# Attention and mixture-of-experts block on one core: the output projection, the next row's k product and VectorE's output sum each placed one head later

## The chip, the cores and the metric

The kernel runs on one core of a Trainium2 chip. The metric is the device time of one execution in microseconds (us). The time of the kernel before is the median of three timed runs; beside it stands one profiled execution, whose trace is what all rows below come from.

## The reference, cut to what matters

The input is x of 8 rows (batch entries) of 256 tokens with 256 features.

```python
x = L0_attn_x                                   # (8, 256, 256)
x = x + layernorm(attn(layernorm(x)))           # 16 heads of 16 features
x = x + layernorm(ffn(layernorm(x)))            # top-1 of 8 experts, and a shared one

def attn(x):
    ct_q, ct_kv = lin(x, w_down_q, b_down_q), lin(x, w_down_kv, b_down_kv)
    q = lin(ct_q, w_up_q, b_up_q) + rope(lin(ct_q, wq_r, bq_r))
    k = lin(ct_kv, w_up_k, b_up_k) + rope(lin(ct_kv, wk_r, bk_r))
    v = lin(ct_kv, w_up_v, b_up_v)
    probs = softmax(q @ k.T / 4)                # per head, 256 x 256
    return lin(probs @ v, wo, bo)               # the output projection
```

What the change touches is the line `lin(probs @ v, wo, bo)` of one row, the layernorm over it, the sum into x and the statistics of the second layernorm, and the down-projection (ct_q, ct_kv) of a later row.

## The kernel before, in words

**Two stages.** The first half of the span is attention, the second half the feed-forward part (shared expert, routed experts, final sums). They overlap only at the seam, in the last row's slot. The change lies in attention.

**Slots and heads.** Attention goes through eight slots, one for each row b (`run_attention`, `run_slot`, lines 378 to 411). A slot has 16 heads, h = 0 to 15. In each slot the engines work on several rows at once, as the table AHEAD (line 317) says: stage B (first layernorm and down-projection) on row b+3, A (q and k, rope) on row b+2, N (v) and the M0 step on row b+1, the scores "SM" and the M1 step on row b+1, the exponentials of the heads themselves on row b, D (output projection, layernorm, sum) on row b-1, E (second layernorm, transposition, router) on row b-2. A step whose row doesn't exist is left out: D is absent from slot 0, B from slots 5 to 7. The last slot (b = 7) is written out by hand in the tables `last` and isn't touched by the change.

**The order is written by hand.** Each engine has a table `order` that maps a head to the steps issued behind it. An engine runs its own list strictly in that order, and the lists meet only in semaphores. TensorE (PE), at each head: the transposed scores of head h (L1535, for the exponentials), the scores "SM" number h for the row maxima (L1476), the steps of `order[h]`, and behind heads 3, 7, 11 and 15 a product of probabilities and v (L1515, `quad`). VectorE (DVE), at each head: the row maximum of SM h (a reduction over a 128x512 bank, L1020, 2 elements out), then its own `order[h]`. ScalarE (ACT): the exponential of head h (L849), then its `order[h]`. GpSimd (POOL) has no work by head, only its steps in order.

**Buffers.** The SM scores go through two banks, so SM u waits until reduction u-2 is done (line 1473). The transposed scores also have two banks, so head h waits for the exponential of head h-2 (line 1533). One bank, w2, is used in turn by the transpositions of the attention output (D_avT0, D_avT1, D_aT), by the output projection D_wo (`d_wo`, lines 1574 to 1579, which adds to `wo_ps`) and by the M0 step. VectorE empties it in `d_wo` (lines 1036 to 1045): the sum with the bias (L1040, adds to `y_ready`), then the statistics (`ln_head`, L954 and L958, and L1044). M0 on TensorE (`m_turn`, lines 1481 to 1498) transposes the split row maxima of row b+1 into the same bank; for rows from 2 on it waits for `y_ready` (line 1494), which is the sum of the same slot.

**What follows the output sum.** The chain goes over three engines: VectorE's sum and statistics (step D_y), GpSimd's power to get 1/sqrt (L620, `D_power` at head 12), VectorE's norm (`d_yn`, L1050, step D_yn), GpSimd's sum into x (L654, `D_x1` at head 13), VectorE's statistics of the new x (`d_stats`, L1054 to L1059, step D_stats), GpSimd's second power (`D_power2` at head 15), VectorE's second norm (`d_xn2`, L1067, step E_xn2, at head 0 of the next slot), and behind it on VectorE the reduction of head 1 and the rope product of row b+2 (`rope`, L988, step A_T at head 1). TensorE needs that rope product for A_QK (L1414 to L1420) at head 2, and the second norm for E_xn2T (L1353) at head 3.

**The M0 path.** M0 on TensorE at head 12, then ScalarE's copy out of the bank (`mT_out`, L832, at head 13) and a small DMA into the stack rows (L835); TensorE waits for that DMA at head 0 of the next slot (line 1529).

**The down-projection.** `a_ct` (B_ct, line 1372) makes the first half (the q side) of the down-projection, `ct_half(b, 1)` (B_ct1) the second; ScalarE's copy of both stands behind head 14.

SyncE issues the DMAs of the q and k stacks and of the expert weights; none of its steps is in the change.

Of the kernel before, what the change touches and what calls it, by code (L numbers as in the profile page):

```python
# [115 lines left out]
def program(nc, x, const, w_down, w_q, w_kv, w_rope, w_out, w_router, bias_col, bias_v, bias_o,  # L116
# [6 lines left out]
    with ExitStack() as ctx:  # L123
# [289 lines left out]
        def nothing(*_):  # L413
            return None
# [509 lines left out]
        def _(dve):  # L924
# [146 lines left out]
            def d_router(b, par):  # L1071
# [7 lines left out]
                "D_div0": divide(0), "D_div1": divide(1), "D_y": d_wo, "D_yn": d_yn, "D_stats": d_stats,  # L1079
                "E_xn2": d_xn2, "E_router": d_router}  # L1080
            order = {0: ("E_xn2",), 1: ("A_T",), 2: ("B_stats",), 3: ("B_norm",), 5: ("E_router",),
                     6: ("D_div0",), 8: ("D_div1",), 9: ("N_v",), 11: ("D_y",),
                     12: ("D_yn",), 14: ("D_stats",)}


            done = [0]
# [257 lines left out]
        def _(pe):  # L1344
# [252 lines left out]
            def d_router(b, par):  # L1597
                pe.wait_ge(sm["xn2T_sb"], b + 1)
                for t in range(TB):
# [7 lines left out]
                     "SM": sm_scores, "M0": lambda b, par: m_turn(b, par, 0),  # L1607
                     "M1": lambda b, par: m_turn(b, par, 1), "D_avT0": av_turn(0), "D_avT1": av_turn(1),
                     "D_aT": a_turn, "D_wo": d_wo, "E_xn2T": d_xn2T, "E_router": d_router}
            order = {0: ("A_R",), 1: ("A_Q",), 2: ("M1", "A_QK",), 3: ("E_xn2T",), 5: ("E_router",),  # L1610
                     6: ("D_avT0",), 8: ("D_avT1", "N_v",), 9: ("D_aT", "B_xnT",), 10: ("D_wo",),
                     12: ("M0", "B_ct",), 13: ("B_ct1",)}

            def ranks(n, par):

# [242 lines left out]
```

## Time and profile before

| what | value |
|---|---|
| timed runs | 449.51, 455.03, 458.82 us (median 455.03) |
| the profiled execution | 447.09 us, with a span of 445.3 us |
| mean granted clock of TensorE in it | 0.979 of full |
| TensorE busy over the span | 414.5 us (93%) |
| VectorE busy | 254.7 us (57%) |
| ScalarE busy | 197.8 us (44%) |
| GpSimd busy | 132.9 us (30%) |

The busy times are means over two stages with different limits: attention ends at about 223 us, and behind it VectorE and ScalarE are much less in use. The granted clock is 1.00 at full speed (2.4 GHz) and 0.50 at the lower level (1.2 GHz). In a timeline row the first number is the start in us from the span's start, the second the duration; a number in brackets is how long the engine sat idle before it and what it waited for. Matmuls overlap, so what a group of them costs is best read from the start of one row to the start of the next.

### The profile page before, as it was taken

To read this page: it belongs to the slowest core of one execution; us is meant where nothing else is said; L and a number is where in the kernel's file an instruction comes from. 1 tells how busy PE (TensorE), PEld (TensorE's weight loads), DVE (VectorE), ACT (ScalarE), POOL (GpSimd) and SP (SyncE) were. 2 spreads that over 40 slices of the span, in tenths; PEclk is the share of its full clock that TensorE was granted. 3 is DMA by queue.
4 is the path that set the end of the run, shared out by engine and by line. 5 is a ranking of instruction groups with operands and counts; after the bars stand their busy time and mean duration, and the time that the engine had idled before them with its cause. 6 is when DMAs were issued, how large, how long until landed. Compare 5 with 4: busy or idle time off the path is not lost.

```text
span 445.3 us, 8888 instructions
## 1 busy us (share of the span) xinstructions
PE 414.5 (93%) x3211; PEld 311.8 (70%) x3211; DVE 254.7 (57%) x601; ACT 197.8 (44%) x375; POOL 132.9 (30%) x186
## 2 busy tenths in 40 slices
PE   6998989999999999797989999999999999999990
PEld 5654656676776767374859999999996344489990
DVE  4655378787878777776655782322222334326685
ACT  1634557667676758556541123444444433211110
POOL 1404231516252524303302002222222010016872
PEclk9998899999999999899999999999999999999996
DMA  8899136364544636350067621111111111113432
GB/s 257 194 99 119 33 90 192 84 189 117 160 143 104 195 88 208 100 170 25 27 208 243 211 73 37 36 49 49 49 47 49 49 47 27 37 52 106 143 99 87
DMA packets 51138, 47.77 MB, mean 107 GB/s; under 512 B 5399, under 2 KB 45847, under 8 KB 51095
## 3 DMA queue, kind: packets, MB, share of 16 engines
q1 hardware_dynamic: 44752, 38.29, 32.3%
q0 software_dynamic: 1728, 4.72, 3.8%
q10 hardware_dynamic: 4614, 4.19, 2.8%
q8 instruction: 26, 0.43, 0.4%
q14 instruction: 18, 0.14, 0.1%
HBM read 25.44 MB, written 8.91 MB: 77 GB/s over the span
## 4 chain that ended last, share of the span: by engine, by line
PE 76%; DVE 10%; issue 5%; POOL 4%; ACT 2%; DMA 2%; DVEq 0%; POOLq 0%; ACTq 0%
PE bank L1349 41%; PE bank L1666 6%; PE bank L1353 6%; PE bank L1515 5%; PE bank L1535 5%; PE bank L1476 4%; PE bank L1683 3%; DVE nmax L1020 2%; PE bank L1414 2%; PE bank L1462 1%; POOL x_sb L654 1%; DVE wall L1050 1%; PE bank L1406 1%; DVE stats_at L954 1%; DMA x_sb<-x 1%
## 5 line engine op out<-in xcount | busy, mean ns | idle before, releaser
L1020 DVE TENSOR_REDUCE nmax<-bank 128x2 f32<-128x512 f32 x112 | 74.3, 685 | 33.4 <-PE bank L1476 33.2
L1226 DVE TENSOR_TENSOR stacks<-stacks,bank 128x512 f32<-128x512 f32 x36 | 24.7, 686 | 69.1 <-PE bank L1349 61.5
L1349 PE MATMUL bank<-stacks,wall 128*128 128x128 f32 x512 | 61.2, 276 | 0.4 <-ACT stacks L885 0.4
L1349 PEld LDWEIGHTS bank<-stacks,wall 128*128 128x128 f32 x512 | 59.8, 192 | 2.5 <-issue 1.8
L849 ACT ACTIVATE pv<-bank 128x512 f32<-128x512 f32 x64 | 38.4, 602 | 36.6 <-PE bank L1535 35.6
L1349 PE MATMUL bank<-wall,stacks 128*128 128x256 f32 (+1 forms) x224 | 53.0, 380 | 0.0
L685 POOL DMA_INDIRECT stacks<-x_sc,row_i x20 | 22.2, 1112 | 100.6 <-PE bank L1353 81.6
L885 ACT ACTIVATE stacks<-bank 128x512 f32<-128x512 f32 x36 | 21.5, 597 | 68.3 <-PE bank L1349 57.3
L849 ACT ACTIVATE wall<-bank 128x512 f32<-128x512 f32 x64 | 38.4, 605 | 29.5 <-PE bank L1535 28.5
L1535 PE MATMUL bank<-stacks 99*128 99x256 bf16 x256 | 49.9, 277 | 0.3 <-DMA stacks<-mT 0.3
L1476 PE MATMUL bank<-stacks 96*128 96x256 bf16 x224 | 42.7, 275 | 7.2 <-DVE nmax L1020 7.2
L1349 PEld LDWEIGHTS bank<-stacks,pv 128*128 128x128 f32 x384 | 44.7, 192 | 1.4 <-issue 0.9
L1349 PE MATMUL bank<-stacks,pv 128*128 128x128 f32 x384 | 44.9, 275 | 0.7 <-ACT stacks L879 0.7
L1349 PEld LDWEIGHTS bank<-wall,stacks 128*128 128x128 f32 x224 | 40.5, 190 | 4.4
L1535 PEld LDWEIGHTS bank<-stacks 99*128 99x128 bf16 x256 | 21.6, 101 | 23.4 <-issue 12.8
L1476 PEld LDWEIGHTS bank<-stacks 96*128 96x128 bf16 x224 | 20.5, 98 | 14.6 <-DVE nmax L1020 11.9
L1666 PE MATMUL bank<-pv,stacks 128*64 128x512 f32 x64 | 30.4, 599 | 0.0
L1666 PE MATMUL bank<-wall,stacks 128*64 x64 | 30.4, 599 | 0.0
L1353 PE MATMUL bank<-cst,wall 128*128 128x128 f32 x160 | 24.0, 276 | 3.2 <-DVE wall L979 2.2
L700 POOL DMA_INDIRECT pv<-y_exp,back_i x16 | 16.1, 1004 | 32.5 <-DMA y_exp<-stacks 28.5
L1353 PEld LDWEIGHTS bank<-cst,wall 128*128 128x128 f32 x160 | 17.9, 140 | 6.8 <-issue 3.8
L894 ACT ACTIVATE pv<-wall 128x1024 f32 x20 | 21.2, 1058 | 3.2 <-DVE eid_i L1204 1.8
(198 smaller groups left out, 699.1 us busy)
## 6 DMA issues: line engine op xcount, KB each, us to landing
wall<-gate_up SPq DMA_DIRECT2D x8, 1024.0 KB, 5.4
stacks<-parts_k SPq DMA_DIRECT2D x72, 64.0 KB, 2.6
stacks<-parts_q SPq DMA_DIRECT2D x72, 64.0 KB, 2.5
wall<-down SPq DMA_DIRECT2D x8, 512.0 KB, 6.7
y_exp<-stacks ACTq DMA_DIRECT2D x20, 128.0 KB, 1.7
x_tok<-wall SPq DMA_DIRECT2D x8, 256.0 KB, 2.5
stacks<-x_tok SPq DMA_DIRECT2D x16, 128.0 KB, 2.6
out<-stacks SPq DMA_DIRECT2D x8, 256.0 KB, 2.1
```

The lines of the kernel that those rows point to most:

```text
L685: pool.indirect_dma_start(out=xl[:, par, :], out_offset=None, in_=x_sc, in_offset=bass.IndirectOffsetOnAxis(ap=row_i[:, s - R0:s - R0 + 1] ...
L849: act.activation(probs[h // QUAD % 2][:, h % QUAD, :], st_bank[h % 2][:, :], ACT.Exp, scale=SCALE).then_inc(sm["exp_done"], 1)
L885: act.activation(sg, fg[:, :], ACT.Silu).then_inc(sm["sg_sb"], 1)
L894: act.activation(to, of, ACT.Copy).then_inc(sm["w_second"], 1)
L1020: dve.tensor_reduce(nmax[:, half, qt, 2 * pair:2 * pair + 2], two(sm_bank[u % 2]), AX.X, ALU.max, negate=True).then_inc(sm["sm_max"], 1)
L1226: dve.tensor_tensor(to, sg, fu[:, :], ALU.mult).then_inc(sm["h_sb"], 1)
L1349: last = pe.matmul(out_ap, lhsT, rhs, start=(n == 0), stop=(n == len(pairs) - 1))
L1353: return pe.transpose(out_ap, in_ap, ident)
L1476: last = pe.matmul(two(sm_bank[u % 2])[:, c, :], stacks[0:ROWS, par, 0, place(h), P * qt:P * qt + P], stacks[0:ROWS, par, 1, place(h), :], ...
L1515: last = pe.matmul(two(av_bank)[32 * c:32 * c + 32, g % 2, :], v_aug[:, par, k, QUAD * g + c, :], probs[g % 2][:, c, S * k:S * k + S], sta ...
L1535: last = pe.matmul(two(st_bank[h % 2])[:, k, :], stacks[0:MROWS, par, 1, place(h), P * k:P * k + P], stacks[0:MROWS, par, 0, place(h), :], ...
L1666: last = pe.matmul((fg, fu)[r][U * n:U * n + U, :], xT[:, p, P * k + U * n:P * k + U * n + U], w, start=(k == 0), stop=(k == KT - 1))
```

## The change

Two `order` tables are edited, TensorE's and VectorE's. No instruction is added, removed or resized, and the tables of ScalarE, GpSimd and SyncE stay as they are.

- TensorE: D_wo from behind head 10 to behind head 11 (the twelfth). B_ct from behind head 12, where it stood after M0, to behind head 13, so that both halves of the down-projection stand together there. M0 stays behind head 12.
- VectorE: D_y from behind reduction 11 to behind reduction 12, D_yn from 12 to 13, D_stats from 14 to 15.

```diff
@@ VectorE @@
             order = {0: ("E_xn2",), 1: ("A_T",), 2: ("B_stats",), 3: ("B_norm",), 5: ("E_router",),
-                     6: ("D_div0",), 8: ("D_div1",), 9: ("N_v",), 11: ("D_y",),
-                     12: ("D_yn",), 14: ("D_stats",)}
+                     6: ("D_div0",), 8: ("D_div1",), 9: ("N_v",), 12: ("D_y",),
+                     13: ("D_yn",), 15: ("D_stats",)}
@@ TensorE @@
-            order = {0: ("A_R",), 1: ("A_Q",), 2: ("M1", "A_QK",), 3: ("E_xn2T",), 5: ("E_router",),
-                     6: ("D_avT0",), 8: ("D_avT1", "N_v",), 9: ("D_aT", "B_xnT",), 10: ("D_wo",),
-                     12: ("M0", "B_ct",), 13: ("B_ct1",)}
+            order = {0: ("A_R",), 1: ("A_Q",), 2: ("M1", "A_QK",), 3: ("E_xn2T",), 5: ("E_router",), 6: ("D_avT0",),
+                     8: ("D_avT1", "N_v",), 9: ("D_aT", "B_xnT",), 11: ("D_wo",),
+                     12: ("M0",), 13: ("B_ct", "B_ct1")}
```

## Rows read from the trace of the kernel before

**Rows 1.** Windows over slot 3: window, its length, busy time by engine, granted clock, DMA.

```profile
110.30:134.00 23.70, 23.13 (x201) 16.50 (x200) 18.91 (x46) 16.29 (x35) 9.68 (x17) 1.00 0.51 147
```

**Rows 2.** Timeline of TensorE, slot 3 from head 10, into slot 4.

```profile
126.02 0.38 PE L1476 MATMUL bank<-stacks 96*128 96x256 bf16 x2
126.24 1.97 PE L1349 MATMUL bank<-wo_sb,wall 128*128 128x256 f32 x8
...
128.27 0.38 PE L1476 MATMUL bank<-stacks 96*128 96x256 bf16 x2
128.58 1.07 PE L1515 MATMUL bank<-wall,pv 128*32 128x256 f32 x16
...
129.81 0.38 PE L1476 MATMUL bank<-stacks 96*128 96x256 bf16 x2
130.13 0.28 PE L1496 MATMUL bank<-idb,mparts 128*24 128x128 bf16 x2
130.34 1.13 PE L1349 MATMUL bank<-wall,wd_sb 128*128 128x256 f32 x4
131.31 0.38 PE L1535 MATMUL bank<-stacks 99*128 99x256 bf16 x2
...
133.05 0.38 PE L1535 MATMUL bank<-stacks 99*128 99x256 bf16 x2
133.71 0.39 PE L1476 MATMUL bank<-stacks 96*128 96x256 bf16 x2 [0.27 <-DVE nmax L1020]
...
135.03 0.39 PE L1535 MATMUL bank<-stacks 99*128 99x256 bf16 x2
...
138.80 0.48 PE L1414 MATMUL bank<-wall,wq_sb 64*128 64x256 f32 x1 [0.33 <-DVE rope_t L988]
```

**Rows 3.** Timeline of VectorE, the same stretch.

```profile
128.69 0.69 DVE L1020 TENSOR_REDUCE nmax<-bank 128x2 f32<-128x512 f32 x1 [1.55 <-PE bank L1476]
129.30 0.68 DVE L1040 TENSOR_TENSOR wall<-bank,bo_sb 128x512 f32<-128x512 f32 x1
...
132.17 0.88 DVE L1050 SCALAR_TENSOR_TENSOR wall<-wall,mv_at,rstd_at 128x256 f32<-128x256 f32 x2 [0.22 <-POOL rstd_at L620]
...
134.43 0.75 DVE L954 BATCH_NORM_STATS2 stats_ff<-x_sb 128x6 f32<-128x256 f32 x2 [0.18 <-POOL x_sb L654]
...
135.68 1.28 DVE L1020 TENSOR_REDUCE nmax<-bank 128x2 f32<-128x512 f32 x2
136.88 0.87 DVE L1067 SCALAR_TENSOR_TENSOR wall<-x_sb,mv,rstd 128x256 f32<-128x256 f32 x2
...
138.27 0.47 DVE L988 SCALAR_TENSOR_TENSOR rope_t<-bank,bcol,cst 128x256 f32<-128x256 f32 x1
```

**Rows 4.** Timeline of GpSimd: the second power of slot 3.

```profile
135.85 0.71 POOL L620 TENSOR_TENSOR rstd<-var_ff,neg_half 128x2 f32<-128x2 f32 x1 [1.46 <-DVE var_ff L1058]
```

**Rows 5.** Chain that ended last, into slot 3: the M0 path's DMA.

```profile
108.85 2.74 DMA stacks<-mT
```

**Rows 6.** Timeline of TensorE: head 15 of slot 0.

```profile
63.88 0.39 PE L1476 MATMUL bank<-stacks 96*128 96x256 bf16 x2 [0.20 <-DVE nmax L1020]
```

**Rows 7.** Timeline of TensorE, slot 6 and the first transposition of slot 7.

```profile
196.29 1.99 PE L1349 MATMUL bank<-wo_sb,wall 128*128 128x256 f32 x8 [0.25 <-ACT wall L856]
...
199.89 0.38 PE L1476 MATMUL bank<-stacks 96*128 96x256 bf16 x2
...
203.78 0.39 PE L1476 MATMUL bank<-stacks 96*128 96x256 bf16 x2 [1.08 <-DVE nmax L1020]
...
207.61 0.66 PE L1353 MATMUL bank<-cst,wall 128*128 128x128 f32 x4 [0.57 <-DVE wall L1067]
```

**Rows 8.** Timeline of VectorE: the output sum of slot 6.

```profile
199.37 0.68 DVE L1040 TENSOR_TENSOR wall<-bank,bo_sb 128x512 f32<-128x512 f32 x1
```

**Rows 9.** Windows behind the waits of slots 5 and 6: clock is the third column from the right.

```profile
181.00:185.00 4.00, 3.78 (x27) 1.74 (x28) 2.82 (x9) 0.92 (x3) 2.32 (x6) 0.57 0.35 87
...
203.80:206.00 2.20, 2.20 (x30) 1.09 (x34) 1.84 (x7) 0.51 (x2) 0.74 (x2) 1.00 0.00 0
```

## The prediction, made before the change was run

> **What bounds the kernel now.** I read the windows by slot first, then the timelines of TensorE, VectorE and GpSimd over one slot, then TensorE's waits and the granted clock. In slot 3 TensorE is busy 23.13 of 23.70 us and VectorE 18.91 [rows 1]: the slot is TensorE's, with little room. Two rows show where it still waits: SM 15 started 0.66 us behind its head (133.05 to 133.71) for reduction 13, 0.44 more than the 0.22 that a pair of score products takes from start to start (126.02 to 126.24), and A_QK in the next slot sat idle 0.33 for the rope product [rows 2]. The second matters more. The rope product is the end of a chain that begins with the output sum and hops over VectorE and GpSimd: sum at 129.30, norm at 132.17 (released by GpSimd), statistics at 134.43 (released by GpSimd), second norm at 136.88, rope at 138.27 [rows 3], A_QK at 138.80 [rows 2]. Slots 1 to 4 are alike in this. So each slot has two paths of nearly equal length, TensorE's own list and this chain, and the change moves the chain's start.
>
> **The change part by part.** No instruction comes or goes, and no DMA is issued by a moved step itself; every cost is a wait.
>
> *D_wo one head later.* Between SM 10 (126.02) and the product behind head 11 (128.58) [rows 2] the same instructions now run in another order: head 11 and its scores, then D_wo. What comes after stays at its times: SM 12 at 129.81, M0 ready to run at 130.13 [rows 2]. Cost by itself 0; SM 11 starts at about 126.46 instead of 128.27, which nobody needs early. VectorE's idle time of 1.55 before reduction 11 [rows 3] doesn't vanish, it moves in front of reduction 12.
>
> *The new wait at M0.* M0 overwrites the bank that the output sum reads, and waits for that sum. Before, the sum ended at 129.98 (129.30 + 0.68) [rows 3], just ahead of M0 at 130.13: hidden. Now the sum is queued behind reduction 12. Reduction 11 started 0.42 behind its scores (128.27 to 128.69) and the sum 0.61 behind that [rows 2, 3]; so reduction 12 starts at 129.81 + 0.42 = 130.23, the sum at 130.84, and it ends at 131.52. With 0.04 to wake an engine (SM 11 ended at 128.65, reduction 11 started at 128.69) M0 runs at 131.56, a stall of 1.43. Its bounds are 0 (the old order) and the 1.43 itself: the statistics behind the sum aren't waited for. Queued behind M0 on TensorE is everything else, head 13 first; for that head ScalarE waits, and for the scores VectorE.
>
> *Both halves at head 13.* B_ct no longer stands behind M0 but behind SM 13. It moves no sum on TensorE in slots 1 to 4, and it lets head 13 and SM 13 start right behind the late M0. ScalarE's copy stands behind head 14 as before: 0. In slot 0, where there is no output sum and two scores run per head, TensorE waits for reductions at the last scores (0.20 at 63.88 [rows 6]); B_ct ran under such waits and now comes behind head 13. Bounds 0 and one half product, 0.97 (130.34 to 131.31 [rows 2]); I take 0.5, the middle, as part of it still lies under waits.
>
> *The M0 path's DMA.* It took 2.74 [rows 5] and head 0 of the next slot waits for it. ScalarE issues it behind the exponential of head 13, which moves from 131.31 [rows 2] to about 131.8 (M0 and its 0.21), so the landing moves by about 0.5, while head 0 moves by 1.43 less the 0.44 that SM 15 no longer waits, 0.99: still hidden.
>
> *The chain from the sum to the rope, in slots 1 to 4.* The sum starts 1.54 later (130.84 against 129.30). The norm follows 2.87 behind the sum and the statistics 2.26 behind the norm, both released by GpSimd [rows 3], so these distances stay: 133.71 and 135.97. The second norm came 2.45 behind the statistics, with two reductions (15 and the next 0, 1.28) in between [rows 3]; now reduction 15 stands ahead of the statistics and one is left, so GpSimd's second power decides: it ended at 136.56 (135.85 + 0.71) [rows 4], 2.13 behind the statistics, so the second norm comes at 135.97 + 2.13 + 0.04 = 138.14. Rope 1.39 and A_QK 1.92 behind that [rows 2, 3]: 140.06 against 138.80, that is **+1.26**. TensorE alone would be there sooner: 1.43 of stall, less the 0.44 at SM 15 and the 0.33 at A_QK, +0.66. The chain is late by 0.60 more, and it decides. Four slots: 5.0. Bounds per slot: 0.66 and 1.43.
>
> *Slots 5 and 6* have no down-projection. D_wo there waited 0.25 for ScalarE; behind head 11 it doesn't, which puts SM 12 at 199.64 instead of 199.89, reduction 12 at 200.06 and the sum at 200.67, against 199.37: 1.30 later [rows 7, 8]. M0 stalls there too, but SM 15, which waited 1.08 for a reduction behind the norm, now gets it before the norm: TensorE wins that back at head 15. It gains nothing by it, since the next slot waits for the second norm at the first transposition, 0.57 idle at 207.61 [rows 7]: with the chain 1.3 later, that is +1.3 from slot 6 to 7. From slot 5 to 6 the old run lost time to the clock (0.57 of full in 181 to 185, a loss of 1.7) [rows 9], and I take 0 there, with bounds of -1.7 (all of that loss) and +1.3.
>
> Sum: 0.5 + 5.0 + 0 + 1.3 = 6.8 us. Behind slot 7 TensorE is busy nearly throughout, so it arrives at the end. The profiled execution of 447.09 would be 453.9. The three timed runs lie higher, at a median of 455.03 with 9.3 between them, and I add the sum to that median: **461.8**, 1.5% slower.
>
> **A rule weighed against the rows.** Behind the two waits of slot 5 TensorE ran at 0.57 of full clock for 4 us, a loss of 1.7; behind the same two waits in slot 6 (203.78 is the second) it stayed at 1.00 [rows 7, 9]. So a wait of about a microsecond can cost the clock or not. The Trainium skill, page "TensorE: Matmul & The Clock Gate", section "A second HAM failure mode: psum-queue depth-cycling", says that short idle times between groups of matmuls, often repeated, make the clock swing between its two levels. The trace agrees in slot 5 and not in slot 6; by the rule each new M0 stall is such a gap, and the result is the first rival below.
>
> **Rivals.**
>
> 1. *The clock falls behind the M0 stalls.* For: slot 5 of before [rows 9]; the stall of 1.43 in one piece is longer than any of the waits there. Against: slot 6, and the long busy stretches on either side of the stall in slots 1 to 4. A drop loses 1.7 us, of which 0.60 lies under the rope's wait: 1.1 for each of four slots, 6.8 + 4.4 = 11.2, time 466.2.
> 2. *Not slower: the rope isn't late.* If the chain's distances of rows 3 shrink because GpSimd and VectorE overlap better than I count (power and norm were both seen waiting), TensorE's list alone decides: 4 x 0.66 = 2.6, slot 0 0.5, and slots 5 and 6 keep up to the 1.08 that TensorE gains at head 15, and slot 5's lost clock of 1.7 comes back: 2.6 + 0.5 - 2.2 - 1.7 = -0.8, time 454.2. It decides once the second norm comes 0.60 earlier than I have it. Against: each hop was released by GpSimd in the rows, and none of these operations changed.
> 3. *Stall without the rest.* If nothing is won back by the waits that go, each slot pays its whole stall: 0.5 + 4 x 1.43 + 2 x 1.3 = 8.8, time 463.8. It is inside the forecast's own range.
>
> **How the numbers follow.** Forecast with rival 3: 0.57, for a time from 459 to 464. Rival 1: 0.22. Rival 2: 0.14. For what I haven't seen: 0.07, of it 0.03 on the fast side. A difference of 2% (9.1 us) is about what a measurement of this kernel can tell from no change. Slower by over 2%: most of rival 1 (0.18), the upper end of the forecast (0.04) and half of the unseen (0.04), 0.26. Faster by over 2%: 0.03. Within: 0.71. The range goes from rival 2 with some of the runs' spread, 453, to above rival 1, 469; the likeliest case's own range is 459 to 464.
>
> **What would show it.** Right: in TensorE's timeline M0 idle some 1.4 us behind SM 12 in slots 1 to 4, released by the sum (L1040); no wait at SM 15; A_QK still waiting for the rope; slots 1 to 4 each 1.3 longer; VectorE idle over 2 in front of reduction 12. Wrong: M0 without a wait, slots as long as before or shorter, or a clock below 1.00 behind the stalls (rival 1).

## The result, and the profile after

The changed kernel took 464.81 us, the median of six runs (456.88 to 468.50); the kernel before, run beside it, 452.33 (six runs, 448.01 to 458.82). The ratio is 1.0221, with a 95% interval from 1.0159 to 1.0283: slower, and whether by more than 2% stays open, since 2% lies inside the interval. The ratios here and below compare only those executions of a kernel that lie within 1.5% of its fastest, so this one is lower than the 1.0276 of the two medians. The forecast was 461.8, with a range from 453 to 469.

The profiled execution has a span of 464.4 us, 19.1 more than before. To see where, I cut both spans at the same instructions. These are TensorE's timeline rows of the kernel before at A_QK (the first L1414 of a slot) in slots 0, 1 and 5 and at the first transposition of slot 6; the one of slot 7 is in [rows 7].

```profile
48.70 0.48 PE L1414 MATMUL bank<-wall,wq_sb 64*128 64x256 f32 x1
...
68.58 0.48 PE L1414 MATMUL bank<-wall,wq_sb 64*128 64x256 f32 x1
...
162.56 0.48 PE L1414 MATMUL bank<-wall,wq_sb 64*128 64x256 f32 x1 [0.33 <-DVE rope_t L988]
...
187.07 0.60 PE L1353 MATMUL bank<-cst,wall 128*128 128x128 f32 x4
```

The same instructions in the changed kernel, with the transposition of slot 7:

```profile
55.13 0.48 PE L1414 MATMUL bank<-wall,wq_sb 64*128 64x256 f32 x1
...
75.59 0.48 PE L1414 MATMUL bank<-wall,wq_sb 64*128 64x256 f32 x1
...
174.42 0.48 PE L1414 MATMUL bank<-wall,wq_sb 64*128 64x256 f32 x1 [0.36 <-DVE rope_t L988]
...
199.52 1.06 PE L1353 MATMUL bank<-cst,wall 128*128 128x128 f32 x4
...
226.71 0.66 PE L1353 MATMUL bank<-cst,wall 128*128 128x128 f32 x4 [0.69 <-DVE wall L1067]
```

| stretch | before | after | more |
|---|---|---|---|
| start to A_QK of slot 0 (ahead of every edited step) | 48.70 | 55.13 | 6.43 |
| to A_QK of slot 1 (the edit in slot 0) | 19.88 | 20.46 | 0.58 |
| to A_QK of slot 5 (the edits in slots 1 to 4) | 93.98 | 98.83 | 4.85 |
| to the first transposition of slot 6 | 24.51 | 25.10 | 0.59 |
| to the first transposition of slot 7 | 20.54 | 27.19 | 6.65 |
| to the end of the span | 237.69 | 237.69 | 0.00 |

The first line isn't the change's: nothing edited has run by then. It and most of the fifth are TensorE's clock, as windows of the changed kernel show (the granted clock is the third column from the right):

```profile
30.00:44.00 14.00, 14.00 (x44) 8.39 (x40) 3.74 (x6) 4.63 (x10) 3.38 (x3) 0.52 0.87 100
...
198.00:212.00 14.00, 13.63 (x80) 8.95 (x81) 6.26 (x12) 4.92 (x9) 1.06 (x6) 0.52 0.50 158
...
222.00:226.00 4.00, 4.00 (x34) 1.36 (x26) 2.82 (x9) 1.81 (x4) 2.16 (x4) 0.60 0.01 3
```

TensorE ran both 14 us stretches at nearly half clock (the 1.2 GHz level), and was busy throughout in one and nearly so in the other. The third row is a shorter fall, of some 3 us, just ahead of the transposition of slot 7. In the profiled execution of before the first two windows stood at 0.90 and 1.00. The stretch from 30 to 44 us comes in traces of other kernels too, among them one that has a single edit far behind it (below), and the profiled execution after happens to have it.

Now the slots themselves. TensorE's timeline of the changed kernel in slot 3, which answers to [rows 2]:

```profile
135.47 0.38 PE L1476 MATMUL bank<-stacks 96*128 96x256 bf16 x2
...
136.13 1.89 PE L1349 MATMUL bank<-wo_sb,wall 128*128 128x256 f32 x8
137.95 1.07 PE L1515 MATMUL bank<-wall,pv 128*32 128x256 f32 x16
138.95 0.39 PE L1535 MATMUL bank<-stacks 99*128 99x256 bf16 x2
139.18 0.38 PE L1476 MATMUL bank<-stacks 96*128 96x256 bf16 x2
141.04 0.27 PE L1496 MATMUL bank<-idb,mparts 128*24 128x128 bf16 x2 [1.47 <-DVE wall L1040]
141.24 0.39 PE L1535 MATMUL bank<-stacks 99*128 99x256 bf16 x2
...
144.08 0.38 PE L1476 MATMUL bank<-stacks 96*128 96x256 bf16 x2
...
149.46 0.48 PE L1414 MATMUL bank<-wall,wq_sb 64*128 64x256 f32 x1 [0.36 <-DVE rope_t L988]
```

M0 (L1496) now sits idle for 1.47 and names the output sum (L1040) as what it waited for. SM 15 (144.08) waits no longer. A_QK still waits for the rope product, as before. VectorE in the same stretch, which answers to [rows 3]:

```profile
139.60 0.69 DVE L1020 TENSOR_REDUCE nmax<-bank 128x2 f32<-128x512 f32 x1 [2.43 <-PE bank L1476]
140.21 0.68 DVE L1040 TENSOR_TENSOR wall<-bank,bo_sb 128x512 f32<-128x512 f32 x1
...
143.09 0.88 DVE L1050 SCALAR_TENSOR_TENSOR wall<-wall,mv_at,rstd_at 128x256 f32<-128x256 f32 x2 [0.22 <-POOL rstd_at L620]
...
145.35 0.75 DVE L954 BATCH_NORM_STATS2 stats_ff<-x_sb 128x6 f32<-128x256 f32 x2
...
147.53 0.88 DVE L1067 SCALAR_TENSOR_TENSOR wall<-x_sb,mv,rstd 128x256 f32<-128x256 f32 x2 [0.23 <-POOL rstd L620]
...
148.93 0.48 DVE L988 SCALAR_TENSOR_TENSOR rope_t<-bank,bcol,cst 128x256 f32<-128x256 f32 x1
```

The idle time in front of the reduction ahead of the sum went from 1.55 to 2.43. From the sum on, the hops are 2.88, 2.26 and 2.18 to the second norm and 1.40 to the rope, nearly as forecast from the old rows (2.87, 2.26, 2.17, 1.39). The whole path from SM 10 to the next A_QK took 12.78 before (126.02 to 138.80) and takes 13.99 now (135.47 to 149.46): 1.21 more.

### The profile page after: what moved, and what is told of

Its sections match the earlier page's. It is cut to its first block, busy times and chain, and to the rows that moved or that the text cites. A ratio compares the mean times of both kernels' runs of the same rounds, so it can differ in the third digit from the quotient of the medians.

```text
span 464.4 us, 8888 instructions
## 1 busy us (share of the span) xinstructions
PE 427.8 (92%) x3211; PEld 320.4 (69%) x3211; DVE 255.8 (55%) x601; ACT 197.9 (43%) x375; POOL 133.1 (29%) x186
## 4 chain that ended last, share of the span: by engine, by line
PE 74%; DVE 9%; issue 7%; POOL 5%; DMA 2%; ACT 1%; ACTq 0%; DVEq 0%; POOLq 0%
PE bank L1349 38%; PE bank L1666 6%; PE bank L1353 6%; PE bank L1515 6%; PE bank L1535 5%; PE bank L1476 4%; PE bank L1683 3%; DMA wkv_sb<-w_kv 2%; PE bank L1414 2%; DVE nmax L1020 2%; POOL x_sb L654 2%; PE bank L1462 1%; DVE wall L1050 1%; DVE stats_at L954 1%; POOL rstd L620 1%
## 5 line engine op out<-in xcount | busy, mean ns | idle before, releaser
L1349 PE MATMUL bank<-stacks,wall 128*128 128x128 f32 x512 | 61.2, 276 | 0.4 <-ACT stacks L885 0.4
L1349 PEld LDWEIGHTS bank<-stacks,wall 128*128 128x128 f32 x512 | 59.8, 192 | 2.5 <-issue 1.8
L1349 PE MATMUL bank<-wall,stacks 128*128 128x256 f32 (+1 forms) x224 | 53.0, 380 | 0.0
L1535 PE MATMUL bank<-stacks 99*128 99x256 bf16 x256 | 51.9, 287 | 0.8 <-DMA stacks<-mT 0.7
L1476 PE MATMUL bank<-stacks 96*128 96x256 bf16 x224 | 43.8, 280 | 3.3 <-DVE nmax L1020 3.3
L1349 PEld LDWEIGHTS bank<-stacks,pv 128*128 128x128 f32 x384 | 44.7, 192 | 1.4 <-issue 0.9
L1349 PE MATMUL bank<-stacks,pv 128*128 128x128 f32 x384 | 44.9, 275 | 0.7 <-ACT stacks L879 0.7
L1349 PEld LDWEIGHTS bank<-wall,stacks 128*128 128x128 f32 x224 | 40.5, 190 | 4.4
L1476 PEld LDWEIGHTS bank<-stacks 96*128 96x128 bf16 x224 | 21.5, 100 | 9.5 <-DVE nmax L1020 6.3
L1353 PE MATMUL bank<-cst,wall 128*128 128x128 f32 x160 | 25.1, 286 | 1.6 <-DVE wall L1067 0.7
L1353 PEld LDWEIGHTS bank<-cst,wall 128*128 128x128 f32 x160 | 19.1, 147 | 5.2 <-issue 2.0
```

Of the source, the lines that this page charges most:

```text
L1349: last = pe.matmul(out_ap, lhsT, rhs, start=(n == 0), stop=(n == len(pairs) - 1))
L1353: return pe.transpose(out_ap, in_ap, ident)
L1476: last = pe.matmul(two(sm_bank[u % 2])[:, c, :], stacks[0:ROWS, par, 0, place(h), P * qt:P * qt + P], stacks[0:ROWS, par, 1, place(h), :], ...
L1535: last = pe.matmul(two(st_bank[h % 2])[:, k, :], stacks[0:MROWS, par, 1, place(h), P * k:P * k + P], stacks[0:MROWS, par, 0, place(h), :], ...
```

## The experiments

Two questions were open: which edit costs the time, the stall at M0 or the chain behind the sum; and whether the clock in slot 6 is the change's doing. The table gives the lengths from A_QK to A_QK, read off TensorE's timeline of each kernel.

| kernel | slot 0 to 1 | 1 to 2 | 2 to 3 | 3 to 4 | 4 to 5 |
|---|---|---|---|---|---|
| before | 19.88 | 22.72 | 23.74 | 23.76 | 23.76 |
| the change | 20.46 | 23.93 | 24.97 | 24.97 | 24.96 |
| VectorE's steps alone | 19.87 | 24.37 | 25.40 | 25.39 | 25.40 |
| TensorE's moves alone | 20.46 | 22.04 | 23.64 | 23.09 | 23.08 |
| M0 behind head 13 | 20.45 | 23.91 | 24.94 | 24.94 | 24.95 |
| down-projection alone | 20.45 | 22.73 | 23.98 | 23.76 | 23.76 |
| statistics back | 20.46 | 24.20 | 25.25 | 25.24 | 25.25 |
| D_wo alone | 19.87 | 22.34 | 23.77 | 23.15 | 23.12 |

**VectorE's three steps alone.**

```diff
-                     6: ("D_div0",), 8: ("D_div1",), 9: ("N_v",), 11: ("D_y",),
-                     12: ("D_yn",), 14: ("D_stats",)}
+                     6: ("D_div0",), 8: ("D_div1",), 9: ("N_v",), 12: ("D_y",),
+                     13: ("D_yn",), 15: ("D_stats",)}
```

> Only VectorE's three steps one head later; TensorE's order as before. Chain theory: the sum is behind reduction 12 all the same, M0 waits 1.5 us in each of slots 1 to 6, and B_ct behind M0 delays the scores of head 13, so that VectorE's norm comes some 0.3 later still: slots 1 to 4 longer by 1.5 each, slot 0 unchanged, in all 7 to 9 us slower. Rival (the moves on TensorE cost the time): slots 1 to 4 within 0.3 of before and the time within 2 us of it.

465.91 us, ratio 1.0367 (1.0332 to 1.0403). Slots 1 to 4 are 1.64 longer, slot 0 isn't, and M0 waits as in the changed kernel. So VectorE's steps bring the cost. They lose 0.43 more per slot than the whole change does. The first half of the down-projection stands between M0 and the scores of head 13 here, and VectorE's timeline in slot 3 shows reduction 13 waiting for those scores, ahead of the norm:

```profile
146.03 0.69 DVE L1020 TENSOR_REDUCE nmax<-bank 128x2 f32<-128x512 f32 x1 [0.57 <-PE bank L1476]
146.64 0.87 DVE L1050 SCALAR_TENSOR_TENSOR wall<-wall,mv_at,rstd_at 128x256 f32<-128x256 f32 x2
```

The norm comes 3.24 behind the sum (143.40) instead of 2.88, which is 0.36 of the 0.43. In time I expected 7 to 9 us more and got 16.4 (465.91 against 449.56 beside it), a miss. Its trace had lost 9.3 ahead of every edit (A_QK of slot 0 at 57.96 against 48.70) and lost 3.1 from the transposition of slot 6 to that of slot 7 (23.68 against 20.54), with half clock in both stretches. So the slots give the price of the edit, and the ratio doesn't.

**TensorE's moves alone.** The `order` table of TensorE from the change, VectorE's as before.

> Only TensorE's moves (D_wo behind head 11, both halves of the down-projection behind head 13); VectorE's order as before, so the sum waits for D_wo right behind reduction 11. Chain theory: the sum starts about 0.7 earlier than before (128.55 in the times of the trace before), M0 doesn't wait, the rope product isn't late, slots 1 to 4 shorter by 0.3 (if the DMA behind M0 then holds head 0) to 0.8, slot 0 longer by 0.6: 0.6 to 2.6 us faster than before. Rival (the moves on TensorE cost the time): 5 us or more slower.

447.61 us, ratio 0.9865 (0.9828 to 0.9903): faster than before, and by more than the 0.6 to 2.6 us expected. With D_wo behind SM 11 reduction 11 comes early, and the sum follows D_wo's end directly. TensorE's moves aren't the cost; one of them gains. VectorE's timeline of this kernel, at the output sum of slot 3, shows that the sum now waits for D_wo (L1349) and no longer for scores:

```profile
131.18 0.69 DVE L1040 TENSOR_TENSOR wall<-bank,bo_sb 128x512 f32<-128x512 f32 x1 [0.88 <-PE bank L1349]
```

Slots 1, 3 and 4 are shorter by 0.67 to 0.68, slot 2 by 0.10 only: a DMA of the next row's stacks holds its end (0.72 idle at 114.46). The expectation left out slots 5 and 6, and more of the gain lies there: 22.64 against 24.51 from A_QK of slot 5 to the first transposition of slot 6, and 19.53 against 20.54 to that of slot 7. A part of the first is the clock that the kernel before lost in its slot 5 [rows 9].

**M0 behind head 13.** The whole change, with M0 moved past the stall:

```diff
-                     12: ("M0",), 13: ("B_ct", "B_ct1")}
+                     13: ("B_ct", "B_ct1", "M0")}
```

> The whole change, but M0 behind the down-projection at head 13 instead of behind head 12, so that the wait for the sum is covered by 1.9 us of work. Stall theory (what TensorE loses at M0 is what the change costs): slots 1 to 4 back to within 0.3 of before, the time 5 to 6 us under the changed kernel. Chain theory (the sum's late start is carried to the rope product): M0 waits for nothing, TensorE is early at head 15, waits about 1.3 more for the rope product, and slots 1 to 4 stay 1.0 to 1.3 longer: the time within 2 us of the changed kernel.

460.11 us, ratio 1.0280 (1.0229 to 1.0331). This is the run that parts stall and chain. TensorE's timeline in slot 3 of this kernel:

```profile
133.93 1.89 PE L1349 MATMUL bank<-wall,wd_sb 128*128 128x256 f32 x8
135.75 0.28 PE L1496 MATMUL bank<-idb,mparts 128*24 128x128 bf16 x2
...
138.88 0.39 PE L1535 MATMUL bank<-stacks 99*128 99x256 bf16 x2 [0.49 <-DMA stacks<-mT]
...
142.88 0.28 PE L1496 MATMUL bank<-idb,mparts 128*24 128x128 bf16 x2 [0.77 <-POOL mparts L648]
143.51 0.48 PE L1414 MATMUL bank<-wall,wq_sb 64*128 64x256 f32 x1 [0.36 <-DVE rope_t L988]
```

M0 at 135.75 waits for nothing; the 1.47 are gone in slots 1 to 4 (in slots 5 and 6, without a down-projection to cover it, 1.03 are left). Yet slots 2 to 4 are 24.94 or 24.95, within 0.03 of the change. The time came back as other waits further on: 0.49 for M0's own DMA at head 0, and 0.77 instead of 0.19 for GpSimd ahead of M1. Behind these A_QK still waits 0.36 for the rope product, as in the change. The chain on VectorE shows why:

```profile
134.29 0.68 DVE L1040 TENSOR_TENSOR wall<-bank,bo_sb 128x512 f32<-128x512 f32 x1
...
137.16 0.88 DVE L1050 SCALAR_TENSOR_TENSOR wall<-wall,mv_at,rstd_at 128x256 f32<-128x256 f32 x2 [0.22 <-POOL rstd_at L620]
...
139.42 0.75 DVE L954 BATCH_NORM_STATS2 stats_ff<-x_sb 128x6 f32<-128x256 f32 x2 [0.18 <-POOL x_sb L654]
...
141.59 0.88 DVE L1067 SCALAR_TENSOR_TENSOR wall<-x_sb,mv,rstd 128x256 f32<-128x256 f32 x2 [0.23 <-POOL rstd L620]
...
142.99 0.47 DVE L988 SCALAR_TENSOR_TENSOR rope_t<-bank,bcol,cst 128x256 f32<-128x256 f32 x1
```

Its hops are 2.87, 2.26, 2.17 and 1.40, within 0.01 those of the change, so A_QK comes no earlier. The stall theory had the slots near 23.75. The stall at M0 is where TensorE loses the time in the changed kernel, and not what fixes the slot's length.

The time by itself would have misled: 460.11 is 4.7 under the 464.84 that the changed kernel took beside it, nearer to what the stall theory said (5 to 6 under) than to the chain theory's 2. In the traces that gain isn't in slots 1 to 4. It lies ahead of every edit (A_QK of slot 0 at 49.27 against 55.13) and from the transposition of slot 6 to that of slot 7 (22.72 against 27.19), and both are stretches with less half clock.

**The down-projection's first half alone, and the statistics back at head 14.**

```diff
@@ on the kernel before @@
-                     12: ("M0", "B_ct",), 13: ("B_ct1",)}
+                     12: ("M0",), 13: ("B_ct", "B_ct1")}
@@ on the changed kernel @@
-                     13: ("D_yn",), 15: ("D_stats",)}
+                     13: ("D_yn",), 14: ("D_stats",)}
```

> Of the change only the down-projection's first half behind head 13. Chain theory: slot 0 is longer by 0.57 as in the changed kernel, slots 1 to 4 within 0.1 of before. Rival (standing behind the stall is what lets the scores of head 13 go first, so the move is worth something by itself): slots 1 to 4 shorter by 0.2 or more.

> The whole change, but VectorE's statistics of the new x stay behind reduction 14. Chain theory: two reductions stand between the statistics and the second norm again, so the norm comes 2.45 instead of 2.17 behind the statistics, as in the trace before, and slots 1 to 4 are longer by a further 0.2 to 0.3. Rival (moving the statistics is a cost of its own): slots 1 to 4 shorter than with the change.

The first took 457.52 in a single execution and made slot 0 longer by 0.57 and three of the four other slots by nothing (slot 2 by 0.24, with a wait of 0.45 for a DMA at its end). It is the whole of slot 0's term, and no gain elsewhere. The second took 465.02, also once; its slots 1 to 4 are 0.28 longer than with the change. That is the difference of 2.45 and 2.17 between statistics and second norm: with two reductions between them the norm is behind VectorE's list, with one behind GpSimd's power.

**The changed kernel again, and with its waits filled.** First the same kernel once more:

> The changed kernel once more, to part what the change does in every execution from what the clock does in some. In the first trace of it TensorE ran at 0.50 from about 31 to 44 us, ahead of every edited step, and again from about 198 to 211 us in slot 6. Theory 1 (chain): slots 1 to 4 are again 1.2 us longer each and slot 0 0.6, whatever the clock does; executions without a long stretch at half clock are 7 to 9 us above those of before without one. Theory 2 (clock): the long stretch in slot 6 comes back in most executions, since the waits ahead of it are the change's own, and the difference is 11 us or more in nearly all of them.

464.84 us (460.87 to 468.31), ratio 1.0312 (1.0242 to 1.0382). The slots came out as in the first trace, 23.92 for slot 1 and 24.95 to 24.96 for slots 2 to 4, as the first theory said. The trace had half clock from about 199 to 213 us again, and all six executions lie 11 us or more above before's 449.56, as the second theory said. But the first six of the change had two at 456.88 and 457.54, with a mean clock of 0.979 and 0.978 against 0.952 in the profiled one. So the long stretch doesn't seem to come every time.

These are TensorE's waits in the changed kernel ahead of that stretch, from M0 of slot 5 on:

```profile
190.61 0.27 PE L1496 MATMUL bank<-idb,mparts 128*24 128x128 bf16 x2 [1.47 <-DVE wall L1040]
...
194.55 0.39 PE L1535 MATMUL bank<-stacks 99*128 99x256 bf16 x2 [0.67 <-DMA stacks<-mT]
...
196.91 0.39 PE L1476 MATMUL bank<-stacks 96*128 96x256 bf16 x2 [0.88 <-DVE nmax L1020]
...
198.37 0.39 PE L1496 MATMUL bank<-idb,mparts 128*24 128x128 bf16 x2 [1.07 <-POOL mparts L648]
```

Next came the change with small matmuls in TensorE's waits, where nothing else is due; their results aren't used:

```diff
+            def fill(n, rows):
+                pe.wait_ge(sm["v_ready"], rows)
+                for _ in range(n):
+                    pe.matmul(w1[:, 0:P], ones_bf[:, :], ones_bf[:, :], start=True, stop=True)
...
             def m_turn(b, par, half):
+                if half == 0 and b >= B - 2:
+                    fill(20, b + 1)
+                if half == 1 and b == B - 2:
+                    fill(14, B - 1)
```

and in the same way 12 ahead of SM 2 and 8 ahead of head 0 of slot 6, and 10 ahead of the first transposition of slot 7.

> The whole change, with small matmuls on constants (128x128, results unused) put into TensorE's waits of slots 5 to 7: 20 ahead of M0, 8 ahead of head 0, 12 ahead of SM 2 and 14 ahead of M1 of slot 6, 10 ahead of the first transposition of slot 7. They add no wait and lie in waits. Clock theory: the stretch at half clock in slot 6 is started by the waits from 189 to 198 us, so it goes, and the time falls by up to 6 us below the changed kernel's in the executions that had it; slots 1 to 4 stay 1.2 longer. Rival (the clock falls there whatever TensorE does, or falls by chance as it does ahead of the edited steps): half clock in slot 6 as often as before, the time the same or longer by the matmuls that don't fit into the waits, up to 3 us.

455.14 us, the median of 11 runs (453.36 to 460.12), ratio 1.0084 (1.0016 to 1.0152). All 11 lie below the six repeats of the change (lowest 460.87), though two of the first six of the change were at 456.88 and 457.54. The slots are the change's (23.93, then 24.96 and 24.97). The window that stood at 0.52, in the profile of this kernel:

```profile
198.00:212.00 14.00, 13.99 (x136) 10.18 (x137) 8.87 (x18) 7.55 (x15) 0.83 (x4) 1.00 0.51 162
```

In this execution too TensorE had the half clock from 30 to 44 us (0.51), which nothing here fills. So with the waits of slots 5 and 6 filled the clock held behind them: by this trace and the 11 times, the stretch at half clock in slot 6 hangs on those waits, while the early one doesn't. First transposition of slot 6 to that of slot 7 takes 21.68 in this kernel (198.83 to 220.51) against 27.19: the half clock costs 5.5 us there, the long stretch and the short one ahead of slot 7 together. The fill moves no data. Its ratio of 1.0084 isn't to be set beside the 1.0312 of the repeat, since the kernel before took 456.56 beside the fill and 449.56 beside the repeat; the times, 455.14 and 464.84, compare better.

The other traces with VectorE's steps late bear this out in part. Each has waits for M0 and the scores at the same place, and each lost the clock there, but not for the same time: some 7 us with the statistics back (0.50 from 199 to 205 us), some 3 with M0 behind head 13 (0.50 from 192.5 to 195.5), twice some 3 with VectorE's steps alone. So the clock fell in all five traces that have these waits unfilled, and how long it falls is left open. Nor are waits in a row enough: the down-projection alone had four at the same place (0.84, 1.09, 0.56 and 0.47, between 187.6 and 194.3), and its clock stood at 1.00 from 187 to 196 us.

**D_wo behind head 11 alone.**

```diff
-                     6: ("D_avT0",), 8: ("D_avT1", "N_v",), 9: ("D_aT", "B_xnT",), 10: ("D_wo",),
+                     6: ("D_avT0",), 8: ("D_avT1", "N_v",), 9: ("D_aT", "B_xnT",), 11: ("D_wo",),
```

> Of the change only D_wo behind head 11; the down-projection and VectorE's steps as before. Chain theory: as with TensorE's moves alone, but slot 0 isn't longer by 0.6: slots 1 to 4 shorter by 0.1 to 0.7 each, no wait at M0, the time 0.5 to 1 us under TensorE's moves alone and 1% or more under before. Rival (D_wo late costs something that the down-projection's move gave back): slots longer than with TensorE's moves alone.

> D_wo behind head 11 alone, a second time, since the interval of the first reached to no change. From its trace (span 441.9 against 445.3, with no half clock behind slot 5): 1% to 1.5% faster than before, the executions without a long stretch at half clock near 443 against 449. Rival (the first result was the chip's state): within 0.5% of before.

The first: 445.21 us, ratio 0.9877 (0.9753 to 1.0002), open at its upper end; the second, with 12 runs: ratio 0.9911 (0.9851 to 0.9970), just short of the 1% to 1.5% expected. The second's median of 451.18 is no better than the 450.72 of before. Two of its executions came near the expected 443 (442.65 and 444.43); the other ten lie from 449.02 to 452.56, and the profiled one of these had the early half clock, ahead of the edit. For the other nine that is only likely, by their mean clock (0.958 to 0.969, against 0.980 and 0.985). So the gain of about 1% is seen in executions without the long early stretch, and they are few.

By the first trace slots 1 to 4 give 1.6 us of the gain and slots 5 and 6 give 2.9 (22.63 against 24.51, 19.53 against 20.54), a part of it the clock that before lost in slot 5. Slot 2 isn't shorter (23.77 against 23.74), which misses the 0.1 to 0.7 expected: two DMA waits, 0.45 and 0.25, stand at its end. TensorE's timeline from slot 3 of the first into slot 4 says what stopped slots 1 to 4 from gaining more:

```profile
134.74 0.39 PE L1535 MATMUL bank<-stacks 99*128 99x256 bf16 x2 [0.25 <-DMA stacks<-mT]
...
138.10 0.48 PE L1414 MATMUL bank<-wall,wq_sb 64*128 64x256 f32 x1
```

A_QK waits for nothing now, and the one wait left is that for M0's DMA at head 0. Against TensorE's moves together I expected 0.5 to 1 us less for leaving slot 0 alone; slot 0 did come back to 19.87, but the two intervals overlap, so which of the two is better stays open.

## Why the prediction was right, and where it was off

- *D_wo one head later, cost 0.* Right, by the runs with TensorE's moves alone. I missed that it can gain: with the sum left at head 11, D_wo's later place frees the reduction ahead of the sum. In the change nothing of that shows, since the sum moves too.
- *The stall at M0.* Forecast 1.43, measured 1.47, in all six slots. That SM 15 then wouldn't wait was right too. That M0's DMA stays hidden was right in slots 1 to 4; head 0 of slot 6 waited 0.67 for it.
- *The chain decides, not the stall.* Forecast +1.26 a slot and 5.0 for four; measured 1.21 and 4.85. The run with M0 moved past its stall shows it: without the stall the slots were as long, and the hops from the sum to the rope the same. Rival 2 (the rope isn't late) and with it "TensorE alone, 0.66" fall. So does rival 3 (1.43 a slot), though its time of 463.8 is the nearest of all to the measured one. "Slots 1 to 4 are alike" wasn't quite so: in the kernel before, A_QK of slot 3 (115.04) waited for nothing, and slot 2 was held by M0's DMA instead (0.30 at 111.64). It got longer by the same 1.23. The credit of 0.28 for one reduction less behind the statistics is confirmed by the statistics moved back.
- *Slot 0.* Forecast 0.5, as the middle of two bounds; measured 0.58, and 0.57 by the down-projection alone.
- *Slots 5 and 6.* Forecast 0 and 1.3. With the waits filled and the clock held they are 0.27 (24.78 against 24.51) and 1.14 (21.68 against 20.54). The 0.27 is two effects that nearly cancel, since the 24.51 of before has the lost clock in it. The down-projection alone, with before's order in slot 5 and the clock at 1.00, took 23.67 there. By that difference the chain costs 1.11 in slot 5 as well, and the lost clock cost before 0.84, not all of the 1.7; the rest lay under waits (0.46 idle ahead of the transposition in before, 0.56 and 0.47 with the down-projection alone).
- *The sum.* 0.58 + 4.85 + 0.27 + 1.14 = 6.8, what was forecast, with some luck in slot 5. The spans are 19.1 apart: 6.8 is this sum, 6.4 the early clock, 5.5 the clock in slot 6 and 0.3 in slot 5. The measured medians are 12.5 apart, so the difference was forecast 5.7 too small. The time came out only 3.0 too small, because the median of 455.03 that the sum was added to was 2.7 above the 452.33 measured beside the change; in that part it was luck.
- *What failed is the weight of rival 1*, "the clock falls behind the M0 stalls", and its place. I gave it 0.22 and put the drops behind each M0 stall of slots 1 to 4, at 1.1 each. There the clock stayed at full in every trace I have. It fell in slot 6, at the end of a row of waits that I hadn't priced: M0 1.47, head 0 0.67, SM 2 0.88, M1 1.07, all between 189 and 198.4 us. I had said of slot 6 only that TensorE "gains nothing by it". A clock below 1.00 behind the stalls was among my own signs of being wrong, and it came, behind the stall of slot 5 and not of slots 1 to 4. The drop lasted 13 us, and with the short one behind it cost 5.5, where I had priced one at 1.7 from the short one of slot 5. The measured time lies within the range all the same, since the range reached above rival 1.
- *The rule on the clock.* The rows agree with the Trainium skill's section "A second HAM failure mode: psum-queue depth-cycling" (page "TensorE: Matmul & The Clock Gate") in part. Short waits close together went with half clock in both traces of the changed kernel and in the three others with VectorE's steps late, and filling them kept it at 1.00; a single wait of 1.47 between long busy stretches didn't bring it down in any slot from 1 to 4. But the four waits with the down-projection alone (0.47 to 1.09) left it at 1.00, so what such a row must be like isn't shown.

Left open: why the fall in slot 6 lasted some 3, 7 or 13 us behind waits that are much alike; and why the early stretch at half clock is long in some executions and short in others. It lies ahead of all that was changed, and the window from 30 to 44 us stood at 0.50 in the second trace of D_wo alone and at 0.91 in the first.

## What to carry to other kernels

Moving a step on one engine moves the start of everything that hangs on its result; add up the hops to the next point where the busiest engine waits, over all engines, before crediting the wait that goes. To tell a stall that costs from one that only shows where the time is lost, move the stalled step and see whether the time comes back as another wait. A row of waits that "costs nothing", because something else ends last, can still cost TensorE its clock for the work behind it.

## What the runs showed of the hardware that I had not expected

TensorE stayed at the lower clock for some 13 us while it was busy throughout (13.63 of 14 us in slot 6, 14.00 of 14 from 30 to 44 us), where the drop of slot 5 in the kernel before lasted under 4 us. Both windows stood at 0.52 over their 14 us. The length of a fall differed more than the waits ahead of it did: in slot 6 it was some 13 us in both traces of the changed kernel, 7 with the statistics back and 3 with M0 behind head 13. And the clock held at 1.00 there when 54 small matmuls on constants (20, 8, 12 and 14, at some 64 to 78 ns each, a group's time over its count) lay in the waits ahead.
